# A vision tower block on one core: the prologue put together anew, with the first two b tables on VectorE

## What is computed

```
dt = exp(log_dt)                                  # (128, 2)
dtL = dt[:, None, 0] * Lambda[None, :, 0] + 1j * (dt[:, None, 1] * Lambda[None, :, 1])
Wc = W * (exp(dtL_neg) - 1) * reciprocal((exp(dtL_neg * 1024) - 1) * Lam)   # the parameters q
h = real(einsum('chn,hnl->chl', Wc, exp(dtL[..., None] * pos - P_max)))     # 64 terms, l < 1024
...
h = h + einsum('bsk,nk->bsn', layernorm(h), weight * block_mask)            # 1024 x 1024
x = layernorm(h)
base = einsum('bsd,od->bso', x, W_base) + b_base                            # 1024 x 1024
weights = sparsemax(einsum('bsd,ed->bse', x, W_router) + b_router)          # 8 experts
hr = einsum('bsd,edr->bser', x, lora_A)                                     # rank 16
h = h + base + einsum('bser,bse,ero->bso', hr, weights, lora_B)
```

## Time and profile before

| what | value |
| --- | --- |
| median of 3 runs | 566.99 us (566.98 to 568.64) |
| span of the profiled execution | 565.1 us |
| PE busy | 509.4 us, 90% |
| PEld (weight load) busy | 426.1 us, 75% |
| DVE busy | 377.0 us, 67% |
| ACT busy | 269.0 us, 48% |
| POOL busy | 100.0 us, 18% |
| DMA | 24.25 MB, 42 GB/s of HBM over the span |

### The profile page before, as it was taken

How to read it: one execution, slowest core, us unless ns; L and a number is a source line. 1 busy time by engine, 2 the same in 40 slices (tenths; PEclk the granted TensorE clock), 3 DMA queues, 4 the chain that set the end, 5 groups by cost and what they waited for, 6 DMA issues and landing times.

```text
span 565.1 us, 7568 instructions
## 1 busy us (share of the span) xinstructions
PE 509.4 (90%) x2609; PEld 426.1 (75%) x2609; DVE 377.0 (67%) x840; ACT 269.0 (48%) x496; POOL 100.0 (18%) x75
## 2 busy tenths in 40 slices
PE   0336889789999999999999999999999999999995
PEld 0325668667888888888888888888888888888884
DVE  5889686789777675767576768676766767642241
ACT  0965876664726363636353544536271717222100
POOL 0693934151010101010100101010101010101010
PEclk9999898899999999999999999999999999999999
...
DMA packets 17244, 24.25 MB, mean 43 GB/s; under 512 B 9352, under 2 KB 11720, under 8 KB 17224
## 3 DMA queue, kind: packets, MB, share of 16 engines
...
## 4 chain that ended last, share of the span: by engine, by line
PE 79%; DVE 9%; POOL 5%; ACT 3%; issue 2%; DMA 0%; SPq 0%; DVEq 0%; POOLq 0%; ACTq 0%
PE acc_b L396 34%; PE acc_a L396 28%; PE turnp L373 5%; PE small L429 4%; PE turnp L389 2%; PE turnp L382 2%; PE small L431 1%; POOL wa_lo L844 1%; PE acc_b L356 1%; DVE v_sb L1016 1%; DVE tmp L1017 1%; PE xps L365 1%; PE acc_b L340 1%; DVE u L1010 0%; DMA kst<-in_consts 0%
## 5 line engine op out<-in xcount | busy, mean ns | idle before, releaser
L874 POOL TENSOR_TENSOR h<-h,bias 128x1024 f32<-128x1024 f32 x16 | 38.4, 2402 | 379.8 <-PE turnp L389 379.8
L396 PE MATMUL acc_b<-wb_hi,x_hi 128*128 128x512 f32 x256 | 88.0, 415 | 0.8 <-DVE wb_lo L964 0.8
L396 PE MATMUL acc_a<-wa_hi,x_hi 128*128 128x512 f32 x256 | 85.0, 408 | 1.9 <-POOL wa_lo L844 1.9
L396 PE MATMUL acc_b<-wb_lo,x_hi 128*128 128x512 f32 x256 | 83.3, 396 | 0.0
L396 PE MATMUL acc_b<-wb_hi,x_lo 128*128 128x512 f32 x256 | 83.1, 395 | 0.0
L396 PE MATMUL acc_a<-wa_lo,x_hi 128*128 128x512 f32 x256 | 82.5, 398 | 0.0
L396 PE MATMUL acc_a<-wa_hi,x_lo 128*128 128x512 f32 x256 | 82.2, 397 | 0.0
L618 ACT ACT_TABLE_LOAD x16 | 20.5, 1283 | 84.4 <-DVE b_sb L1037 83.1
L396 PEld LDWEIGHTS acc_a<-wa_hi,x_lo 128*128 128x128 f32 x256 | 48.6, 190 | 11.8
L396 PEld LDWEIGHTS acc_a<-wa_lo,x_hi 128*128 128x128 f32 x256 | 48.6, 190 | 11.5
L396 PEld LDWEIGHTS acc_b<-wb_hi,x_lo 128*128 128x128 f32 x256 | 48.5, 189 | 11.6
...
## 6 DMA issues: line engine op xcount, KB each, us to landing
...
```

The costliest lines, as they stand in the source:

```text
L396: return pe.matmul(cols, a, rows, start=first, stop=last)
L874: pool.tensor_tensor(h2[par][:, :], h2[par][:, :], bias[:, :], ALU.add).then_inc(bias_added, 1)
```

## The change

It touches the prologue, and two places of the loop.

- **Parameters in two rounds.** The exponential is taken on the two columns of `log_dt` as they are (`dt_exponential`), TensorE spreads the result over the partitions (`dt_transposes`), and `dec_and_turn` makes the products with Lambda from PSUM. `ROUNDS` splits the heads into the first 16 and the other 112. Each round has its `q_arguments(r)`, its tanh and sines, its two reciprocals and its `parameters(r)`, the first of which ends ahead of table v(0) and the second ahead of table v(2). The scratch columns now lie in `lb_raw` and `bias`, whose loads wait for the second round.
- **Centring.** W_base, lora_A and the router's weight stay as they are: `wb_sums`, `wb_centre`, `cat_means` and the subtraction on VectorE go. In their place ScalarE takes the mean off `h2` itself in every tile, ahead of its transposes (`h2_centre`), and GpSimd adds it again in `add_bias` (L881), so that this has two passes. Of w_attn the tiles from 2 on are centred by GpSimd.
- **Low parts of w_attn.** GpSimd makes those of tiles 1, 3, 4 and 6 (`BY_POOL`), VectorE those of 0, 2, 5 and 7.
- **The b tables.** b(0) and b(1) are made by VectorE, right behind v(0) and v(1). b(2) stays with GpSimd.
- **Queues.** The constants, Lambda, the first tile of x and the router's weight come in on ScalarE's DMA queue. Tile 0 is split into `x2_hi` and `x2_lo`, and the others, as all before, into `x1_hi` and `x1_lo`. The halves 0 and 1 of W_base are transposed around `k_transposed(1)`, ahead of attention(1), and 2 to 15 between the products of both first attentions; `base(0)` runs in one piece, with `k_transposed(2)` in its first part and `k_rows(2)` behind it.

```diff
-P_ARGS = 20
-Q_NORM = 10
+DT_STEPS = 14
+ROUNDS = (slice(0, 2 * HT), slice(2 * HT, H))
+ARG_STEPS, Q_NORM, Q_STEPS = 2, 10, 12
...
-        CENTRE_LAST, DIRECT = NWT // 2 + 1, NWT // 2
+        BY_POOL = (1, 3, 4, 6)
+        CENTRE_LAST = 2
...
+            def dt_transposes():
+
+                pe.wait_ge(consts_in, 16)
+                pe.wait_ge(dt_step, DT_STEPS)
+                for r in range(2):
+                    mm = pe.transpose(small[:, r * P:(r + 1) * P], dt_p[:, r:r + 1].to_broadcast([P, P]), ident)
+                mm.then_inc(dt_t, 1)
...
+            def h2_centre(t, par):
+
+                s = st2[:, par, :]
+                act.wait_ge(h2_ready, t + 1)
+                act.activation(s[:, 1:2], s[:, 0:1], ACT.Copy, scale=-1.0 / L).then_inc(h2_mean, 1)
+                act.wait_ge(h2_mean, t + 1)
+                act.activation(h2[par][:, :], h2[par][:, :], ACT.Identity, bias=s[:, 1:2]).then_inc(h2_centred, 1)
...
-            parameters()
-            table_b(0)
-            wa_lows(0)
+            parameters(0)
+            wa_centre(2)
+            wa_centre(3)
+            wa_centre(4)
+            wa_lows(3)
...
-            table_b(1)
-            for j in range(NWT):
-                wb_centre(j)
-            table_b(2)
+            wa_lows(6)
+            parameters(1)
...
+            table_b(2)
...
+                pool.tensor_tensor(h2[par][:, :], h2[par][:, :], st2[:, par, 1:2].to_broadcast([P, L]), ALU.subtract)\
+                    .then_inc(mean_added, 1)
+                pool.wait_ge(mean_added, t + 1)
...
+            reciprocal_of_norm(0)
             mask_sums(5)
             wa_mask(4)
+            wa_lows(2)
+            table_v(0)
+            table_b(0)
             mask_sums(6)
+            q_arguments(1)
             wa_mask(5)
-            decay_b(1)
-            k_low(0)
-            wa_lows(8)
-            wa_lows(9)
+            phases(1)
             mask_sums(7)
             wa_mask(6)
-            wa_lows(10)
-            wa_lows(11)
+            k_low(0)
             wa_mask(7)
-            for i in range(12, 2 * NWT):
-                wa_lows(i)
+            wa_lows(5)
             table_v(1)
+            table_b(1)
+            wa_lows(7)
...
-            phases(3)
-            wb_lows(LATE + 3)
...
+            decay_b(2)
+            h2_low(0)
+            for i in range(12, 2 * NWT):
+                wb_lows(i)
+            phases(3)
+            h2_reciprocal(0, 0)
+            h1_reciprocal(1)
```

More of the change, by code:

```diff
@@ L190, in build_vit_tower @@
         cat_raw = wr_raw[:, :, 1, :]
-        slot = [b[:, 2 * H * i:2 * H * (i + 1)] for b in (flat(b_sb), tmp) for i in range(4)]
+        slot = [b[:, 2 * H * i:2 * H * (i + 1)].rearrange("p (s h) -> p s h", s=2)
+                for b in (lb_raw, bias) for i in range(4)]
         def block_bank(j):
@@ L546, in _ @@
                 if k == 2:
+                    k_transposed(2)
+                if k == KC // 2:
                     x_transposes(3)
-                if k == KC // 2:
-                    k_rows(2)
                 if k == KC - 2:
                     gated_transpose(0)
-                base(0, k, (1,))
+                base(0, k)
+            k_rows(2)
             pe.wait_ge(lorb_lo, 1)
@@ L628, in exp_and_sin @@
                     .then_inc(tab_sin, 1)
+            def exp_and_sin(t):
+                exponentials(t)
+                sines(t)
             def k_high(t):
@@ L728, in _ @@
-            k_copy(1)
-            wb_sums(6)
-            h2_high(0)
-            wb_sums(7)
-            exp_and_sin(2)
-            wb_highs(6)
-            wb_highs(7)
-            wb_highs(8)
-            wb_highs(9)
-            k_deviation(1)
+            exponentials(2)
+            for i in range(5, 9):
+                wb_highs(i)
+            sines(2)
+            wb_highs(9)
+            h2_centre(0, 0)
+            k_copy(1)
+            act.wait_ge(lora_in, 16 * KC)
+            act.wait_ge(rt_copied, 1)
@@ L801, in parameters @@
                 link(pool.tensor_tensor(d_i, d_i, w1, ALU.add))
-                m0, m1 = two(slot[1])[:, 0], two(slot[1])[:, 1]
+                m0, m1 = start[1], end[1]
                 pool.tensor_tensor(m0, d_r, d_r, ALU.mult)
```

468 lines of the change are left out of this document (233 added, 235 removed).

## The result

| kernel | median, us | range of its runs | against before |
| --- | --- | --- | --- |
| before | 566.99 | 566.64 to 568.64 | |
| changed | 554.38 | 552.86 to 554.81 | 0.9767 (95%: 0.9748 to 0.9786) |

A forecast was written before the change was run, and what follows sets the result against it. TensorE bounds the loop at 29.6 us a tile, so the prologue only shifts its start. The walked queues, corrected by 2.2, put k_transposed(3) at 141.1 against 143.36: 566.99 - 2.2 = 564.8 us, range 557 to 571.

The forecast's parts named there:

- What bounds the kernel: Loop: TensorE is busy throughout at 29.6 us a tile, so a prologue change only moves when that rhythm begins.
- Cost: nothing: Loop and tail: h2 centring and GpSimd's second pass, at most 2.4 us, fit under 3.0 us of slack.
- Rival D: Loop: GpSimd's new pass lasts longer than 3 us; at 4.4 it costs 15 us in all, 580 us; chance 0.05.
- Start and table v(0): Prologue start: q chain 7.7 us, v(0) from 30.2 meeting two GpSimd instructions, k_transposed(0) at 43.3 against 45.74.
- First attention and the idle time behind it: Prologue: first attention at 55.5 against 59.90, then TensorE idles 7.3 us for w_attn's last low parts behind b(1).
- Attention(1) to the gates: Prologue: attention(1) at 88.1, base(0) at 106.9, phases(3) losing 7.4 us beside GpSimd, gates at 121.0.
- From the gates to the loop: Prologue end: TensorE waits 3.8 us for the gates, then finishes base(0), k_rows(2) and experts; loop begins at 128.2.
- The correction: k_transposed(3): the walk over the old queues was 2.2 us too slow, so 143.3 becomes 141.1, a 2.2 us gain.
- A: Prologue, faster: GpSimd's instructions block VectorE less and the q chain is shorter, 6.9 us less, 558 us; chance 0.25.
- B: Prologue, slower: the second q chain loses 6.3 us alternating with VectorE, tables come 4.4 later, 569.2 us; chance 0.21.
- C: Prologue: VectorE's tensor_scalar of 256 columns also waits for GpSimd, 0.8 us later, 565.6 us; chance 0.08.
- The rule of the prediction: VectorE: an instruction with two SBUF inputs stands until the running GpSimd instruction ends, about one wait per GpSimd instruction.

The follow-up runs named there:

- after_again: The changed kernel as it is, run again beside three padded kernels on one chip: 553.59 us.
- before_x1024: The kernel before with cat and 128 unused bytes moved in front of x1_hi, so x tiles lie a multiple of 1024 bytes behind the weights: 559.32 us.
- pad_after_x: The changed kernel with 32 unused bytes in front of x1_hi: 560.89 us.
- after_pool_waits: The changed kernel with GpSimd waiting for the gates of tile 0 before lora_B's low part, the mean and the bias: 550.76 us.
- after_all64: The changed kernel with 64 unused bytes in front of all its tiles, weights and x tiles moving together: 555.40 us.
- pad_before_x: The kernel before with 32 unused bytes in front of x1_hi: 564.75 us.
- after_x64: The changed kernel with 64 unused bytes in front of x1_hi: 561.37 us.
- after_x256: The changed kernel with 256 unused bytes in front of x1_hi: 555.23 us.
- after_b_pool: The changed kernel with b(0) and b(1) made by GpSimd again, beside tables v(0) and v(1): 557.59 us.
- after_low_first: The changed kernel with w_attn's last low parts ahead of b(1) on VectorE, and TensorE's order around k_transposed(1) turned: 552.46 us.

## Right and wrong, by the steps of the prediction

**What bounds the kernel.** "The loop and the tail follow it one for one, unless they get a new wait of their own" was wrong, and it is the step that cost most. They got no new wait, but their products got a new pace, 29.03 us a step instead of 29.63, and between kernels that differ in placement alone this is worth 7.8 to 8.3 us of the whole. "Cost: nothing" for the loop was right for what it spoke of: GpSimd's second pass lasts 1.90 us, both together 4.3, and after_again steps in 29.03 us where before_x1024, without the pass and without `h2_centre`, has 29.08. Rival D falls. The part of the change that moved the loop was not a line of work at all but a constant that became smaller. Taken off, the change gained 5.7 us, nearly all of it in the prologue, where 2.2 were forecast.

**Start and table v(0).** k_transposed(0) was forecast at 43.3 and came at 43.00, by two errors against each other. GpSimd's chain took 7.4 us (7.7 forecast), but began at 19.8 and not at 17.8, since ScalarE's tanh and sines came later, and v(0) began at 32.0 instead of 30.2; v(0) and b(0) then met one GpSimd instruction and not two. The chain's first and last instruction:

```profile
19.81 0.24 POOL L797 TENSOR_TENSOR bias<-bias 128x32 f32<-128x32 f32 x1 [19.38 <-ACT bias L582]
...
27.00 0.22 POOL L833 TENSOR_TENSOR qi<-bias,lb_raw 128x16 f32<-128x16 f32 x1
```

**First attention and the idle time behind it.** 55.29 against 55.5, and a wait of 6.56 against 7.3: right, mechanism and size. Of b(1)'s waits for GpSimd, 3.7 forecast, about 2.8 came: it took from 62.60 to 69.6.

**Attention(1) to the gates.** 86.60 against 88.1, base(0) at 105.35 against 106.9, the gates' transpose at 118.42 against 121.1. Of the first 1.5 us, 0.9 is b(1)'s. The placement adds next to nothing here: from attention(1) to base(0) after_again takes 18.73 us and pad_after_x, with its x tiles displaced, 18.83. phases(3) was forecast to lose 7.4 us and began 1.6 us earlier than thought; it took 9.0, so 6.6 were lost. after_pool_waits shows the term itself: 9.0 us with GpSimd beside, 3.1 without.

**From the gates to the loop.** 7.1 us had been set, 5.27 came. My walk let TensorE run at half speed behind its wait for the gates, and here it didn't: the granted clock was 1.00 in all of 116 to 124. In other executions it did, and the same stretch took 6.85 us (next section).

**The correction.** The walk was 2.2 us too slow over the old queues (2.9 at the start of the loop, 2.1 at k_transposed(3)), and I took the same off the new one. It was 5.2 too slow there (143.3 against 138.12). The error was not a constant. Its largest parts in the new queues are 1.8 us of half clock from the gates to the loop, 0.9 at b(1) and 0.8 at phases(3), and none of them is the same for old and new queues. The first is partly luck: in after_all64, where the half clock did come, k_transposed(3) starts at 139.30, 1.2 us later than here. Taking the constant off is the second step that failed, and the one that made the prologue's 5.2 us look like 2.2.

**The rivals.** A named the right side for the wrong reason: nothing blocks less. B fell, the second round of q was ready at 89.3 and nobody waited. C was right as a mechanism: the `TENSOR_SCALAR` of 256 columns at 108.63 took 1.87 us beside GpSimd, and 0.29 with GpSimd idle (in after_pool_waits at 105.69). The Trainium skill, SBUF — State Buffer, section Who interferes with whom, which says that VectorE in a 2-port mode, tensor_scalar among the instructions that can enter it, contends with GpSimd, agrees with this row. Its price was probably small, since the step before and the step behind waited too; no run has this wait alone.

## What the runs showed of the chip

**The distance of the stationary from the moving operand.** Products of 128 x 128 by 512 columns start 0.227 to 0.228 us apart in the changed program where the x tile lies a multiple of 256 bytes behind the weights, 0.232 at 128 bytes beyond (pad_before_x), 0.233 at 32 and 64, and 0.234 to 0.235 at 96 (before); the exception is `acc_b` in the old program, 0.230 at 0 mod 256 (before_x1024, above). For other shapes nothing follows. `k_transposed` lasts 1.95 us in all kernels, but its two operands, `v_sb` and `b_sb`, keep their distance in all of them. The router takes 1.92 to 1.94 us, but its weight rows are 1088 bytes apart, so that its distances mod 256 change from product to product wherever x lies. Whether the distance from each weight tile counts or one common grid can't be told, since all weights lie multiples of 256 from each other.

**The clock behind a wait of 2.1 to 2.6 us.** After the wait ahead of k_transposed(3), 2.1 to 2.4 us in all kernels with the new prologue, TensorE goes on at full speed in some executions and at half in others. The windows of after_again and of after_x64 (us, busy of PE, PEld, DVE, ACT, POOL, granted clock):

```profile
140.00:144.00 4.00, 4.00 (x26) 3.55 (x25) 1.14 (x2) 3.99 (x9) 0.00 (x0) 1.00 0.00 0
```

```profile
140.00:144.00 4.00, 4.00 (x25) 4.00 (x23) 2.70 (x7) 3.96 (x9) 0.00 (x0) 0.61 0.00 0
```

A clock of 0.61 is a mean of full speed and half. The step it lies in takes 31.9 us in the first kind and 33.3 to 33.6 in the second (after_all64 33.36, after_x256 33.37, after_b_pool 33.39, after_pool_waits 33.37, after_low_first 33.25, with the pace of 29.03 in all later steps), so it costs 1.4 to 1.7 us.

The same happens behind the wait for the gates. The timeline of PE, and the window of 118 to 123, in after_again and then in after_all64:

```profile
118.01 0.33 PE L442 MATMUL small<-kst,hw_sb 128*128 128x128 f32 x1 [2.62 <-DVE hw_sb L1118]
...
123.28 1.09 PE L403 MATMUL turnp<-kst,h 128*128 128x128 f32 x8
...
118.00:123.00 5.00, 4.99 (x27) 4.20 (x27) 4.32 (x10) 2.49 (x5) 0.00 (x0) 1.00 0.00 0
```

```profile
118.03 0.33 PE L442 MATMUL small<-kst,hw_sb 128*128 128x128 f32 x1 [2.60 <-DVE hw_sb L1118]
...
124.88 1.09 PE L403 MATMUL turnp<-kst,h 128*128 128x128 f32 x8
...
118.00:123.00 5.00, 4.97 (x18) 3.96 (x19) 4.32 (x10) 1.51 (x3) 0.00 (x0) 0.66 0.00 0
```

The waits are 2.62 and 2.60 us, and the same work then takes 5.27 us in the one and 6.85 in the other; after_x64, after_x256, after_b_pool and pad_after_x are of the second kind too. The two places together, 3.1 us, are as much as the runs of this kernel differ (552.18 to 555.65 over all its placements at 0 mod 256), and single executions, or medians of four from different chips, can't be compared to less. What decides it stays open; the waits ahead were alike.

**VectorE beside GpSimd.** The rule of the prediction held in each place shown here. A step of VectorE with both inputs in SBUF took up to 2.6 us where it met a GpSimd instruction of 1024 columns (1.9 to 2.6 us long), and ended within 0.3 us of it.

**To carry over.** Before a prologue is tuned, look at the pace of the steady products and at where their two operands lie to each other: a smaller constant moved them by accident and was worth more than the whole rebuild. A move from a busy engine to another pays only if the first doesn't fill the gap with work that the second waits for, so ask what comes next in its queue. And a calculation that is off on the old kernel is not mended by a constant, if its errors sit in mechanisms that the change has more of.
